# Four unrolled head groups of a state-space stage rolled into a loop on each engine, and weight splits moved ahead of a layer norm's casts

## The reference, cut to what matters

```python
x = x + attn_a(layernorm(x))   # state-space heads, called stage A here
x = x + ffn(layernorm(x))      # shared FFN and 16 experts, top 4
x = x + attn_b(layernorm(x))   # 16 heads of gated linear attention, stage B
x = x + ffn(layernorm(x))
```

```python
CB = einsum('blhn,bmhn->bhlm', C_c, B_c)
M  = CB * exp(where(mask, cum_l - cum_m, -inf))
Y  = M @ val + einsum('blhn,bhdn,blh->bhld', C_c, h, exp(cum)) + D * val
```

## Time and profile before

| what | value |
| --- | --- |
| median of 3 runs | 1495.89 us |
| profiled execution | 1496.01 us |
| its span | 1494.2 us |
| PE busy | 1437.9 us (96%), 8520 products |
| DVE, ACT, POOL busy | 897.2, 863.9, 817.1 us |
| stage A with its norm | 0 to about 443 us |
| first FFN, stage B, second FFN | from about 443, 703 and 1227 us |
| mean granted TensorE clock | 0.989 of full |

### The profile page before, as it was taken

How to read it: one execution, slowest core, us unless ns; L and a number is a source line. 1 busy time by engine, 2 the same in 40 slices (tenths; PEclk the granted TensorE clock), 3 DMA queues, 4 the chain that set the end, 5 groups by cost and what they waited for, 6 DMA issues and landing times.

```text
span 1494.2 us, 24410 instructions
## 1 busy us (share of the span) xinstructions
PE 1437.9 (96%) x8520; PEld 1248.1 (84%) x8520; DVE 897.2 (60%) x1713; ACT 863.9 (58%) x1735; POOL 817.1 (55%) x685
## 2 busy tenths in 40 slices
PE   7799999999999999999999999999999999999998
PEld 5589898898976778887789999999999987778886
DVE  6776766767664443434766767677666754443434
ACT  5566666666655343333677777777777755343332
POOL 4744444444434555553576666766676634555553
PEclk9999999999999999999999999999999989999999
DMA  2133332332311111111232123212222011111111
GB/s 83 32 66 79 68 69 67 67 78 68 69 53 32 43 43 53 42 53 32 65 82 63 51 57 74 63 49 56 63 63 63 15 42 33 43 42 53 42 53 39
DMA packets 48603, 82.48 MB, mean 55 GB/s; under 512 B 4256, under 2 KB 29984, under 8 KB 48288
## 3 DMA queue, kind: packets, MB, share of 16 engines
q1 hardware_dynamic: 48544, 81.70, 21.1%
HBM read 80.38 MB, written 1.31 MB: 55 GB/s over the span
## 4 chain that ended last, share of the span: by engine, by line
PE 58%; issue 5%; ACT 5%; DVE 4%; POOL 4%; DMA 0%; DVEq 0%; POOLq 0%; ACTq 0%; SPq 0%
PE ps L243 19%; PE ps L245 18%; PE ps L244 18%; POOL planes_lo L393 1%; POOL ms_b_lo L393 1%; ACT q L1317 1%; POOL qk_lo L393 1%; PE ps L294 1%; PE ps L301 1%; DVE qsum L1455 1%; ACT planes_hi L1322 1%; DVE f_h L1081 0%; DMA fw_raw<-ffn_w 0%; ACT qk_hi L389 0%; ACT fh_hi L389 0%
## 5 line engine op out<-in xcount | busy, mean ns | idle before, releaser
L393 POOL TENSOR_TENSOR ms_a_lo<-m_a,ms_a_hi 128x384 fp32r<-128x384 f32 x128 | 129.9, 1015 | 200.2 <-ACT ms_a_hi L389 200.2
L1081 DVE TENSOR_TENSOR f_h<-f_sc,ps 128x512 f32<-128x512 f32 x112 | 76.4, 682 | 182.5 <-POOL f_sc L1013 182.5
L243 PE MATMUL ps<-xn_hi,fgu_hi 128*128 128x512 f32 x448 | 177.3, 396 | 5.2 <-DVE f_h L1081 5.2
L245 PE MATMUL ps<-xn_hi,fgu_lo 128*128 128x512 f32 x448 | 178.2, 398 | 0.0
L244 PE MATMUL ps<-xn_lo,fgu_hi 128*128 128x512 f32 x448 | 177.0, 395 | 0.0
L1083 DVE TENSOR_TENSOR fh_lo<-f_h,fh_hi 128x512 fp32r<-128x512 f32 x112 | 107.2, 957 | 98.3 <-ACT fh_hi L389 98.3
L962 ACT ACTIVATE f_s<-ps 128x512 f32<-128x512 f32 x112 | 66.7, 597 | 161.2 <-PE ps L245 161.0
L1013 POOL TENSOR_TENSOR f_sc<-f_s,coef_r 128x512 f32<-128x512 f32 x88 | 114.0, 1296 | 67.5 <-ACT f_s L962 67.5
L389 ACT CAST fh_hi<-f_h 128x512 fp32r<-128x512 f32 x112 | 69.1, 617 | 124.9 <-DVE f_h L1081 124.8
L393 POOL TENSOR_TENSOR fd_lo<-fw_raw,fd_hi 128x256 fp32r<-128x256 f32 x56 | 52.1, 930 | 125.7 <-ACT fd_hi L389 125.7
L243 PE MATMUL ps<-xn_hi,aw_hi 128*128 128x512 f32 x256 | 108.8, 425 | 7.4 <-DVE bmat_lo L696 7.4
(11 more groups left out here) (276 smaller groups left out, 4901.1 us busy)
## 6 DMA issues: line engine op xcount, KB each, us to landing
fw_raw<-ffn_w SPq DMA_DIRECT2D x56, 384.0 KB, 3.0
rows_a<-a_rows_d SPq DMA_DIRECT2D x64, 256.0 KB, 4.8
wconv_raw<-b_conv SPq DMA_DIRECT2D x16, 513.0 KB, 3.6
aw_raw<-a_heads SPq DMA_DIRECT2D x32, 256.0 KB, 5.2
wvo_raw<-b_vo SPq DMA_DIRECT2D x16, 512.0 KB, 3.6
rows_b<-b_rows_d SPq DMA_DIRECT2D x32, 256.0 KB, 4.8
wqk_raw<-b_qk SPq DMA_DIRECT2D x16, 256.0 KB, 4.8
x<-xT SPq DMA_DIRECT2D x2, 512.0 KB, 4.9
```

The source lines that it names most:

```text
L243: nc.tensor.matmul(o, w[0], v[0], start=first, stop=False, skip_group_check=True)
L245: return nc.tensor.matmul(o, w[1], v[0], start=False, stop=last, skip_group_check=True)
L393: return nc.gpsimd.tensor_tensor(dst[1], src, f32(dst[0]), ALU.subtract).then_inc(sem(done_sem), 1)
L1081: nc.vector.tensor_tensor(f_h[:, c], f_sc[:, c], ps[:, 2 + c, :], ALU.mult).then_inc(sem("f_h"), 1)
```

## The change

Two edits. In `norm_act`, `prepare_first(act)` is called once ahead of the casts of both chunks, right behind the two square roots, instead of between the casts of chunk 0 and chunk 1. In stage A, the first three calls of each group function become one `Fori` of three turns on each of the five engines, and the fourth (with `last` true) stays behind it as its own copy.

```diff
             for c in range(CHUNKS):
                 act.wait_ge(sem("ln_v"), CHUNKS * n + c + 1)
                 nc.scalar.activation(norm_cols(ln_s, c), norm_cols(ln_v, c), ACT.Sqrt).then_inc(sem("ln_std"), 1)
+            prepare_first(act)
             for c in range(CHUNKS):
                 for k in range(KT):
                     act.wait_ge(sem("ln_xn"), KT * (CHUNKS * n + c) + k + 1)
                     nc.scalar.copy(xn[0][:, k, cols(c)], ln_xc[:, k, cols(c)]).then_inc(sem("ln_hi"), 1)
-                if c == 0:
-                    prepare_first(act)
             prepare_rest(act)
@@ a_dve, and in the same words a_pe, a_act, a_pool, a_sp
-            for g in range(A_TILES):
-                a_group_dve(dve, g, g == A_TILES - 1)
+            with dve.Fori(0, A_TILES - 1) as g:
+                a_group_dve(dve, g, False)
+            a_group_dve(dve, A_TILES - 1, True)
```

More of the change, by code:

```diff
@@ L418, in a_pe @@
             a_state_pe(pe, 0, 0)
-            for g in range(A_TILES):
-                a_group_pe(pe, g, g == A_TILES - 1)
+            with pe.Fori(0, A_TILES - 1) as g:
+                a_group_pe(pe, g, False)
+            a_group_pe(pe, A_TILES - 1, True)
             for n in range(4):
@@ L558, in a_act @@
             act.wait_ge(sem("a_ncum"), 1)
-            for g in range(A_TILES):
-                a_group_act(act, g, g == A_TILES - 1)
+            with act.Fori(0, A_TILES - 1) as g:
+                a_group_act(act, g, False)
+            a_group_act(act, A_TILES - 1, True)
             for c in range(CHUNKS):
@@ L790, in a_pool @@
             nc.gpsimd.memset(lo[:, VALZ - VPAD:part], 0.0).then_inc(sem("valz_zero"), 1)
-            for g in range(A_TILES):
-                a_group_pool(pool, g, g == A_TILES - 1)
+            with pool.Fori(0, A_TILES - 1) as g:
+                a_group_pool(pool, g, False)
+            a_group_pool(pool, A_TILES - 1, True)
         def a_group_pool(pool, g, last):
@@ L814, in a_sp @@
                 sp.dma_start(rows_a[:, c], rows_of(a_rows_d, 0, c)).then_inc(sem(f"a_rows_loaded{c}"), 16)
-            for g in range(A_TILES):
-                a_group_sp(sp, g, g == A_TILES - 1)
+            with sp.Fori(0, A_TILES - 1) as g:
+                a_group_sp(sp, g, False)
+            a_group_sp(sp, A_TILES - 1, True)
         def a_group_sp(sp, g, last):
```

## The result

The changed kernel takes 1513.43 us in the median of four runs (1512.18 to 1514.98), the kernel before 1495.95 in the same session. The ratio is 1.0114 (95% interval 1.0097 to 1.0132): slower by 17 us. The profiled execution has 1511.5 us and a span of 1509.7 us. Of the ten executions of run e9 further down two were far slower (1763.61 and 2836.32 us): its median of 1502.60 us is of all ten, that of the other eight is 1501.58, and its ratio is of the eight.

The account below looks back on a forecast made before the run. PE, busy 96% of the span, was taken to bound the kernel. Against the profiled 1496.0 us, -0.5 + 0.2 + 5.0 + 1.7 = +6.4 gave 1502.4, 1502.3 against the median; range 1494.3 to 1506.5 for 8 in 10.

Parts of the forecast that it names:

- The fetch: Stage A's two backward branches: DVE's target block is missing and refetched, 2.5 us on the chain each, +5.0 us.
- the second rival: Stage A boundaries: DVE and PE blocks both miss, or DVE fetches twice in a row; clock falls twice; 1509 us, chance 0.08.
- What comes late at 160.89 comes late at 166.43 by as much: Stage A group boundary: a delay of DVE's exponent bounds reaches PE's first value product in full.
- The clock: Stage A boundaries: PE idle over 3 us, so its clock falls once for the two, +1.7 us, ends 0 and 3.4.
- The moved call: Layer norms: earlier casts shorten PE's wait, against contention; -0.5 at each FFN, +0.5 ahead of stage B, sum -0.5 us.
- Register work: Stage A loops: waits and addresses in registers, two backward branches and the entry, +0.2 us, ends 0 and +1.0.
- the third rival: Faster: blocks held, norms give their best, no clock fall in the norm ahead of stage B; 1489.7 us, chance 0.06.
- the boundary as the place: Stage A group boundary: where another engine's cost can reach PE, through a chain from DVE to PE without slack.
- PE's target as held: Stage A loop: PE's body of 1273 instructions, five blocks, finds its branch target still in its deep store.
- packets on q14 behind both backward branches: Sign of the forecast: q14 packets at both ends of turns in stage A, near 160 and 256 us.
- The wait before the first value product: Sign at stage A's boundaries: this PE wait grows from 0.49 to about 3 us, but not at the third.
- The first rival: No block is missing at the backward branches; only -0.5 + 0.2 remain, 1495.6 us, chance 0.36.

Follow-up runs that it names:

- e9: The whole change plus eight more DVE instructions at the program's start, against the kernel before: 1502.60 us against 1497.67, ratio 1.0032.
- e5: Stage A loops on all five engines, no moved call, eight more DVE instructions at the program's start, against the kernel before: 1497.79 us against 1496.79, ratio 1.0011.
- e6: Stage A loops alone, with 2 or 40 more DVE instructions at the start, against the kernel before: 1509.06 us (ratio 1.0081) with 2, 1505.00 us (1.0056) with 40.
- e1: The moved call alone, stage A unrolled, against the kernel before: 1500.48 us, ratio 1.0022.
- e2: The stage A loops alone on all five engines, prepare_first as before, against the kernel before: 1509.01 us against 1496.79, ratio 1.0083.
- e4: Stage A loops on PE, ACT, POOL and SP only, DVE unrolled, prepare_first as before, against the kernel before: 1497.69 us against 1497.66, ratio 0.9998.
- e7: Stage A unrolled, only the weight PE's first product needs cast early, between the norm's square roots, against the kernel before: 1493.05 us against 1497.66, ratio 0.9971.

## Why the prediction was wrong

The direction was right (slower, 0.57), the size was not: 1502.3 us was forecast, with a range up to 1506.5, and 1513.4 came. The mechanism of the loop was the forecast one. Two terms of the sum were mis-sized, and a third had the wrong sign.

**The fetch, +5.0 forecast, +7.9 measured.** A single missing block costs about what was assumed: 2.8 us was taken for it and 0.3 for branch and registers, and the trace has 2.9 from branch to target, of which 0.3 is there without a fetch (e5). But two are missing in a row. The forecast wrote that the body starts at DVE's 63rd instruction and that the blocks change near the 67th, and did not draw the conclusion; it stood under the second rival with a chance of 0.08 ("DVE needs two fetches in a row, since it leaves the first block after a few instructions"). e6 with 2 and with 40 instructions showed it to be this. PE's wait grew from 0.49 us to 4.33 and 4.58, together 4.33 + 4.58 - 2 × 0.49 = 7.9 us, against 2 × 2.5 in the sum. The delay reached PE another way than forecast. "What comes late at 160.89 comes late at 166.43 by as much" does not hold: the first group is 5.15 us longer from `m_a` to `m_a`, but PE had other products to do till 166.80, so its wait grew by 3.84.

**The clock, +1.7 forecast, +3.4 measured.** Two falls instead of one, each 3.5 to 3.6 us at 0.52 to 0.53 of full. PE's idle time of over 4 us at both boundaries comes from the first error, and after every wait of about 4 us or more in these runs the clock fell.

**The moved call, -0.5 forecast, +3.3 measured.** This is the step that failed in kind: the gain was set above the contention. The forecast saw the contention and named its price (an `xn_lo` beside POOL takes about 1.0 us longer), but put it behind the gain: it noted that POOL's new work "falls beside DVE's `ln_diag`" and took one instruction slowed in front of PE and one behind as the worst case (+0.8), with half the gain as the middle. Two DVE instructions in a row are held, and the first of them is a step of 4 columns, which loses as much as a wide one, because what it pays is the rest of POOL's instruction. POOL's next one starts at 466.75, 0.1 us ahead of `ln_diag`, so the second is held too. That is 1.07 and 1.03 us, 2.1 us against 1.05 us of gain (PE waits for `xn_lo` instead of `rw_lo`), at each of three norms. Ahead of stage A three are held: 0.52, 1.03 and 1.02 us beyond their usual time, and the `xn_lo` of chunk 0 as well; of the 3.0 us there about 0.8 reach stage A's first `m_a` (e1).

The Trainium skill, page "SBUF — State Buffer", section "SBUF: two separate sides", gives the exclusive lock for the whole instruction. The trace agrees to 0.02 us: `ln_r` ended at 466.81, POOL's `rw_lo` at 466.79. The prediction cited the rule and let it change "the ends, not the middle"; it should have set the middle.

**Register work, +0.2 forecast.** Where no fetch covers it, a group is 0.5 us longer at a backward branch (e5: 93.98 and 93.95 for 93.45). In the changed kernel it lies inside PE's waits above. The third group's 0.4 us cannot be read as register work, since the second fall of the clock lies in that group.

Together: stage A's groups have 11.2 us (7.9 of waits and 3.4 of clock make 11.3), and the moved call has 3.3: 14.5 us, the low end of the ratio's interval. The ratios of e1 and e2 add to 15.7. Of the remaining one to three microseconds no run shows the place. The profiled executions differ in two things that no edit explains. One is how late the first norm begins: its second square root came at 15.04 us before, at 15.25 to 16.73 in the other kernels, and in the changed one (16.59) the first transfers, `x` and the constants, took 5.5 and 6.5 us to land for 4.9 and 5.6. The other is where the clock falls elsewhere: the fall at 718 us is not in the changed kernel, as the third rival had it, but one at about 514 us is there that the kernel before does not have.

What was right: the boundary as the place, DVE as the engine whose blocks are missing, PE's target as held, the third boundary as free, and packets on q14 behind both backward branches as the sign (they start at 163.5 and 262.4 us here, near 160 and 256 in the forecast). The wait before the first value product, also named as a sign, did not come. The first rival (nothing is missing) would have come true with the body eight instructions further on; its argument, that 356 instructions are over twice 166, was the wrong count. What decides is how many blocks a turn touches. Whether DVE holds four blocks and fetches one of them ahead, or three besides the one under way, the runs do not tell apart.

The Trainium skill, page "Runtime: NRT & Kernel Launch", section "Instruction fetch mechanics", lets a branch miss whose target lies outside a window of two pages. Its pages are of 16 KiB. Here the target in e5 lies about 356 instructions behind the branch, nearly three blocks of 8 KB, and is held; on PE it lies nearly five blocks of 16 KB behind (e4) and is held too. The measurement decides. The 32 KiB that the section gives for most engines agree: four blocks of 8 KB, one of which was fetched ahead.

## What to carry to other kernels

Before rolling a long body into a loop, count the blocks of instructions that one turn touches on each engine, with its start's place in a block, and compare with what that engine holds; on DVE here four blocks of 128 instructions were held, the one fetched ahead included, and a turn that touched five left DVE idle for up to 4.9 us at its branch. Where it is just over, a few instructions more ahead of the loop's entry can be worth more than a saved instruction (eight of them gained 11.2 us): look for the branch, the start of its target, and packets on the instruction queue between. Work given to POOL is to be placed against DVE's critical steps instruction by instruction, narrow steps included: the price here was the rest of POOL's instruction, for a step of 4 columns and one of 512 alike, and one early split in a place with slack (e7) beat both kernels.

## What the runs showed of the hardware that was not expected

- A DVE instruction on 4 columns that began 0.05 us behind a POOL instruction of 1.27 us took 1.23 us for 0.16.
- PE's body of 1273 instructions had no packet at backward branches (none on q8 in e5 from 150 to 345 us); DVE's of 356 fetched five blocks a turn or none, depending on where it started (ten packets in the changed kernel from 150 to 345 us, none in e5).
- PE's clock stayed at full speed after a wait of 2.49 us and fell to its lower level after one of 2.22 us in the same execution.
